# Whole score maxima in four steps over three banks, two score banks, and a reordered routing tail

## The chip, the cores and the metric

The kernel runs on one core of one Trainium2 chip, in one launch. The metric is the device time of that launch in microseconds (us); lower is better. All tensors are float32.

## The reference, cut to what matters

There are 2 sequences of 1024 tokens with 256 features, and a context of 77 tokens for each. The input is normed and is the source of the latents; here the queries come from the 1024 tokens, and the keys and values from the 77 context tokens together with the 1024 tokens, 1101 keys in all. There are 16 heads of 64.

```
q = lat @ Wq ;  k, v = split(concat([x, lat]) @ Wkv)
attn = softmax(q k^T * 64**-0.5) ;  x = x + (attn @ v) @ Wout
xn = layernorm(x)
shared = (silu(xn @ sg) * (xn @ su)) @ sd
scores = l2norm(xn) @ l2norm(centroids).T        # 8 groups, 32 experts
experts of the best 4 groups, of these the best 4 (+ bias), gates = softmax of their scores
routed = sum over the 4 experts of gate * FFN_e(xn), each expert taking its first 320 tokens
out = x + shared + routed
```

## The kernel before

**Numbers in two halves.** Most products are taken in a fast float32 form (F32R) with each operand split into a high part, written by ScalarE (a Copy), and a low part, written by VectorE (a subtraction). A product is then three matmuls: high by high, high by low, low by high.

**Blocks.** The attention runs in 8 turns `T` of 4 blocks `d`: a block is a pair of heads (`pp = d // 2`) with 512 queries (`d % 2`). A turn handles two head pairs of one sequence. Inside a block each of the two heads `h` has 9 slots, one for each 128 keys (`kt`). A slot `("st", d, h, kt)` is two matmuls into a bank of `ps_st` (L906, L910); ScalarE takes the exponential out of the bank (L1569), and GpSimd adds it to a running sum of the row (`add`, L725). The second score matmul also brings in minus the maximum of each query's row. `ps_st` has three banks, used in turn, so a score waits for the exponential of three scores before.

**Maxima.** The maximum over all 1101 keys has to be known before a head's first score. So the scores of that head are computed once more ahead, in 6 steps `("max", d, h, i)`: two matmuls of 370 keys by 128 queries into the two banks of `ps_m` (L883), and one VectorE reduction of 2 x 369 values into two columns of `piece_max` (L1279). There are 12 pieces for a head, three to each 128 queries. A step waits until the reduction of the step before has emptied both banks (`max_done`). `("neg", d, h)` reduces the 12 partial maxima to 4 (L1285), and `("row", d, h)` turns them into a row with a matmul (L889) and a masking on VectorE (L1292). The second head's maxima are taken in the first half of its own block (`own_max`), the next block's first head's in the second half (`next_max`).

**Order of the work.** Every engine walks one list, `PLAN`, which `whole_plan()` writes out by hand, and issues its own part of each event, in that order; semaphores tie the parts together. `turn_slots()` gives the events after each slot of a block: the projections of the next head pair (`k`, `q`, with their `hi` parts on ScalarE and `lo` parts on VectorE), `v`, the products with the values (`av`, L921), the row sums (`sum`, L928, and a VectorE reciprocal, L1296), the norm on GpSimd (`norm`, L730) and the output product (`out`, L941). Blocks with odd `d` project keys (`project`), those with even `d` only the next queries. `extra_events()` puts the work of other stages in: second sequence, and the norm, scores and routing of token groups 0 and 1, spread over VectorE.

**Two more banks.** All other products that leave TensorE go through a ring of two banks, `ps_t`: job number `jn` uses `ps_t[jn % 2]`, and `bank_free`, `job_filled` and `job_done` wait on its two pairs of semaphores. Together this is 2 + 3 + 1 (`ps_o`) + 2 banks, all eight.

**The tail.** After the last block come four chunks of 512 tokens of the shared FFN (`up` into `ps_m` and `ps_st`, `silu` on ScalarE, `hid`, `lowh` on VectorE, `down`), and between them the routing of token groups 2 and 3: norms (`norm_a`, `norm_b`), transposes (`turned`), `score`, `top`, `mask`, `best`, `hot`, `pos`, `places`, and 16 scatters of rows each on GpSimd (`scat`, L742). In the order before, all of group 2's routing and the start of group 3's lie before `("down", 0)`. Behind the list, SyncE waits for the scatters and loads the first expert's rows (`feed(0, 0, False)`); TensorE transposes them (`turn_rows(0, 0)`, L986). Then the loop over 32 experts runs, each an `up` (L780) and a `down` (L817, L811).

Of the kernel before, what the change touches and what calls it, by code (L numbers as in the profile page):

```python
# [12 lines left out]
P = 128  # L13
# [31 lines left out]
MAX_STEPS = 6  # L45
# [3 lines left out]
def turn_slots():  # L49
# [3 lines left out]
    for d in range(QUADS):  # L53
# [8 lines left out]
        def own(*ev):  # L62
            return ev, 0
# [10 lines left out]
        def project_k(i):  # L74
# [7 lines left out]
        own_max = [own("max", d, 1, i) for i in range(MAX_STEPS)] + [own("neg", d, 1)]  # L82
        next_max = [nxt("max", n, 0, i) for i in range(MAX_STEPS)] + [nxt("neg", n, 0)]
        out = [old("out", prev, i) for i in range(2)]
        after = {(0, 1): own_max[1:2],
                 (0, 4): own_max[4:5],
                 (0, 6): own_max[5:],
                 (0, 8): [own("row", d, 1), next_max[0], old("sum", prev)],
                 (1, 1): [],
                 (1, 2): [old("norm", prev), next_max[1]],  # L90
                 (1, 3): first_values + [next_max[2]],
                 (1, 4): [out[0], next_max[3]]}
        if project:
            after[0, 0] = [own_max[0]] + project_k(0)
            after[0, 1] += [k_low[0]]
            after[0, 2] = project_k(2) + [own_max[2], k_low[2]]
            after[0, 3] = project_k(1) + [own_max[3], k_low[1]]
            after[0, 5] = project_q() + [q_again] + last_values + [q_low]
            after[1, 5] = [nxt("v", pp, 0), next_max[4]]
            after[1, 6] = next_max[5:] + more_values + [nxt("row", n, 0), out[1]]  # L100
# [19 lines left out]
def extra_events():  # L120
# [84 lines left out]
    put(30, 1, 7, "end", ("ws", 0))  # L205
    c(31, ("wl", 0))
    put(31, 0, 6, "end", ("wload", 1))
    put(31, 1, 5, "end", ("ws", 1))
    put(31, 1, 6, "end", ("wl", 1), ("wload", 2))
    put(31, 1, 7, "end", ("stat_a", 2), ("stat_b", 2))  # L210
# [4 lines left out]
def whole_plan():  # L215
# [5 lines left out]
              ("max", 0, 0, 1), ("max", 0, 0, 2), ("v", 0, 1), ("max", 0, 0, 3), ("max", 0, 0, 4), ("v", 0, 2),  # L221
              ("max", 0, 0, 5), ("neg", 0, 0), ("row", 0, 0)]
# [4 lines left out]
    for T in range(TURNS):  # L227
        for slot in slots:
            more = extra.get((T,) + slot[0][0][1:], [])
            for n, (ev, back) in enumerate(slot):  # L230
                place = "row" if ev[0] == "row" else "mid" if n == len(slot) - 1 else None
                plan += [(new, T) for at, new in more if at == place]
                if 0 <= T - back < TURNS:
                    plan.append((ev, T - back))
                elif T == 0 and ev[0] == "out":
                    plan.append((("cen", ev[2]), 0))
# [11 lines left out]
    def last(c):  # L248
        return [("high", c, HIDS - 1), ("lowh", c, HIDS - 1), ("down", c), ("accout", c)]

    tail = av + [("up", 0, 0), ("norm_a", 2), ("norm_b", 2), total, ("silu", 0, 0), ("up", 0, 1), ("turned", 2, 0),
                 ("turned", 2, 1), ("hid", 0, 0), norm, ("silu", 0, 1), ("low", 2, 0), ("low", 2, 1), ("hid", 0, 1),
                 ("ws", 2), ("wl", 2), ("norm_c", 2), ("up", 0, 2), ("score", 2), ("scored", 2)] + outs
    tail += [("silu", 0, 2), ("high", 0, 0), ("lowh", 0, 0), ("hid", 0, 2), ("stat_a", 3), ("stat_b", 3), ("root", 3),
             ("high", 0, 1), ("lowh", 0, 1), ("top", 2), ("up", 0, 3), ("mask_a", 2), ("mask_b", 2), ("silu", 0, 3),
             ("hid", 0, 3), ("high", 0, 2), ("lowh", 0, 2), ("norm_a", 3), ("norm_b", 3), ("best_a", 2), ("best_b", 2),
             ("turned", 3, 0), ("turned", 3, 1), ("high", 0, 3), ("lowh", 0, 3), ("hot_a", 2), ("hot_b", 2),
             ("hot_c", 2), ("gexp", 2), ("low", 3, 0), ("low", 3, 1), ("norm_c", 3), ("pos", 2), ("score", 3),
             ("gates", 2), ("places_a", 2), ("places_b", 2), ("scored", 3)] + scats[2]
    tail += [("down", 0), ("accout", 0)] + hidden(1, 0) + [("top", 3), ("mask_a", 3), ("mask_b", 3)] + hidden(1, 1)  # L260
    tail += [("best_a", 3), ("best_b", 3), ("gexp", 3), ("hot_a", 3)] + hidden(1, 2) + [("hot_b", 3), ("hot_c", 3)]
    tail += hidden(1, 3) + [("pos", 3), ("gates", 3), ("places_a", 3), ("places_b", 3)] + scats[3] + last(1)
    tail += hidden(2, 0) + hidden(2, 1) + hidden(2, 2) + hidden(2, 3) + last(2)
    for ht in range(HIDS):
        tail += hidden(3, ht) + ([("ws1", ht)] if ht < WPIECES else [])
    tail += last(3)
# [3 lines left out]
JOB_KINDS = ("k", "q", "v", "row", "sum", "out", "cen", "zt", "turned", "score", "pos")  # L270


def xattn_moe(nc, x, ctx_in, ln_m_g, ln_m_b, ln_l_g, ln_l_b, Wq, Wkv, Wout, group_c, expert_c, e_bias,
# [33 lines left out]
    jobs = 0  # L307
    for ev, T in PLAN:
        if ev[0] in JOB_KINDS:
            JOB[ev, T] = jobs  # L310
            jobs += 1
# [6 lines left out]
    PADS = jobs % 2  # L318
    TURNED_IN = [T for ev, T in PLAN if ev[0] == "turned" and ev[2] == DT - 1]
    J_EXPERT = jobs + PADS  # L320
# [18 lines left out]
    with ExitStack() as stack:  # L339
# [194 lines left out]
        def exp_of(T, d, h, kt):  # L534
            return T * ST_T + SCORES.index(("st", d, h, kt)) + 1 + 3
# [1136 lines left out]
```

## Time and profile before

| | us |
|---|---|
| median of 3 runs | 1708.82 (1708.56 to 1709.96) |
| the profiled execution | 1708.1 |
| its span, first to last instruction | 1706.4 |
| TensorE matmul busy | 1520.7 (89%) |
| VectorE busy | 1053.5 (62%) |
| ScalarE busy | 797.0 (47%) |
| GpSimd busy | 936.3 (55%) |

The attention blocks fill 54 to 1165 us of the span, the tail 1165 to 1284, and the expert loop the rest. TensorE matmuls are pipelined: a row's duration overlaps with the next row's, so the pitch from start to start is what one costs. A bracket at the end of a row is the idle time of the engine before it, with what ended it.

### The profile page before, as it was taken

To read this page: it belongs to the slowest core of one execution; us is meant where nothing else is said; L and a number is where in the kernel's file an instruction comes from. 1 tells how busy PE (TensorE), PEld (TensorE's weight loads), DVE (VectorE), ACT (ScalarE), POOL (GpSimd) and SP (SyncE) were. 2 spreads that over 40 slices of the span, in tenths; PEclk is the share of its full clock that TensorE was granted. 3 is DMA by queue.
4 is the path that set the end of the run, shared out by engine and by line. 5 is a ranking of instruction groups with operands and counts; after the bars stand their busy time and mean duration, and the time that the engine had idled before them with its cause. 6 is when DMAs were issued, how large, how long until landed. Compare 5 with 4: busy or idle time off the path is not lost.

```text
span 1706.4 us, 24003 instructions
## 1 busy us (share of the span) xinstructions
PE 1520.7 (89%) x8086; PEld 1070.6 (63%) x8086; DVE 1053.5 (62%) x1770; ACT 797.0 (47%) x1501; POOL 936.3 (55%) x747
## 2 busy tenths in 40 slices
PE   3798999998989989899899998987789999999995
PEld 3465555555555556555565555544678999999995
DVE  6556666576565656667666676565645666666662
ACT  3344444444444435544354443444225566666663
POOL 4456666666565665666557677784432343333433
PEclk8899999999999999999999999998798999999998
DMA  3032440000000000000001010111225676666664
GB/s 99 12 77 68 89 97 10 23 14 10 14 10 23 14 10 23 14 10 14 10 23 30 26 31 23 30 45 56 72 92 176 171 196 166 184 181 167 192 170 93
DMA packets 99283, 117.94 MB, mean 69 GB/s; under 512 B 10595, under 2 KB 78181, under 8 KB 99173
## 3 DMA queue, kind: packets, MB, share of 16 engines
q1 hardware_dynamic: 82149, 96.97, 19.4%
q0 software_dynamic: 17056, 19.97, 6.0%
q8 instruction: 44, 0.72, 0.2%
q14 instruction: 34, 0.28, 0.0%
HBM read 74.93 MB, written 35.06 MB: 64 GB/s over the span
## 4 chain that ended last, share of the span: by engine, by line
PE 67%; DVE 17%; POOL 6%; ACT 6%; issue 2%; DMA 0%; SPq 0%; POOLq 0%; DVEq 0%; ACTq 0%
PE ps_o L921 10%; DVE piece_max L1279 9%; PE ps_t L780 9%; PE ps_m L780 8%; PE ps_m L883 8%; PE ps_st L780 8%; POOL arena L725 5%; PE ps_st L906 4%; PE ps_t L941 4%; PE ps_st L910 3%; PE ps_st L817 2%; PE ps_o L817 2%; ACT arena_r L1546 2%; PE ps_t L986 2%; PE ps_t L889 2%
## 5 line engine op out<-in xcount | busy, mean ns | idle before, releaser
L725 POOL TENSOR_TENSOR arena<-arena 128x512 f32<-128x512 f32 (+1 forms) x512 | 662.0, 1294 | 388.9 <-ACT arena L1569 350.7
L1569 ACT ACTIVATE arena<-ps_st 128x512 f32<-128x512 f32 (+1 forms) x576 | 328.0, 597 | 492.3 <-PE ps_st L910 473.2
L1279 DVE TENSOR_REDUCE piece_max<-ps_m 128x2 f32<-128x738 f32 x384 | 353.2, 920 | 223.9 <-PE ps_m L883 221.3
L755 POOL DMA_INDIRECT acc_rows<-arena,ids x96 | 150.7, 1570 | 291.2 <-ACT arena L1629 263.5
L883 PE MATMUL ps_m<-arena_r 128*128 128x370 f32 x768 | 220.4, 368 | 76.5 <-DVE piece_max L1279 69.9
L921 PE MATMUL ps_o<-arena 128*64 128x512 f32 (+1 forms) x1152 | 272.3, 608 | 0.0
L906 PE MATMUL ps_st<-arena_r 128*128 128x512 f32 (+1 forms) x576 | 242.1, 420 | 0.7 <-ACT arena L1569 0.7
L883 PEld LDWEIGHTS ps_m<-arena_r 128*128 128x128 f32 x768 | 130.2, 191 | 175.2 <-DVE piece_max L1279 148.6
L910 PE MATMUL ps_st<-arena_r 68*128 68x512 f32 (+2 forms) x576 | 229.7, 399 | 0.4 <-DVE arena_r L1292 0.4
L921 PEld LDWEIGHTS ps_o<-arena 128*64 128x64 f32 (+1 forms) x1152 | 75.1, 138 | 145.1 <-issue 138.1
L780 PE MATMUL ps_m<-arena_r 128*128 128x320 f32 (+1 forms) x864 | 163.9, 325 | 1.2 <-DVE arena_r L1431 1.2
L780 PE MATMUL ps_st<-arena_r 128*128 128x320 f32 (+1 forms) x864 | 160.2, 321 | 0.0
L906 PEld LDWEIGHTS ps_st<-arena_r 128*128 128x128 f32 (+1 forms) x576 | 107.2, 186 | 60.6 <-issue 51.7
L780 PEld LDWEIGHTS ps_m<-arena_r 128*128 128x128 f32 x864 | 135.8, 190 | 12.3 <-issue 8.5
L780 PEld LDWEIGHTS ps_st<-arena_r 128*128 128x128 f32 x864 | 138.0, 190 | 4.1
L1419 DVE TENSOR_TENSOR arena<-arena,ps_st 128x320 f32<-128x320 f32 x128 | 61.9, 484 | 126.1 <-ACT arena L1604 126.1
L1405 DVE TENSOR_TENSOR arena_r<-arena,arena_r 128x1024 fp32r<-128x1024 f32 x93 | 113.7, 1222 | 15.8 <-ACT arena_r L1591 12.5
L910 PEld LDWEIGHTS ps_st<-arena_r 68*128 68x128 f32 (+2 forms) x576 | 107.0, 186 | 11.8 <-DVE arena_r L1292 1.4
L780 PE MATMUL ps_t<-arena_r 128*128 128x512 f32 x384 | 105.9, 413 | 7.1 <-DVE arena_r L1269 5.2
L1296 DVE RECIPROCAL arena<-ps_t 128x512 f32<-128x512 f32 x32 | 106.8, 3337 | 1.2 <-PE ps_t L928 1.2
L1604 ACT ACTIVATE arena<-ps_m 128x320 f32<-128x320 f32 x128 | 56.4, 440 | 103.5 <-PE ps_st L780 101.3
L1591 ACT ACTIVATE arena_r<-arena 128x1024 fp32r<-128x1024 f32 x93 | 98.4, 1058 | 0.0
(183 smaller groups left out, 1859.3 us busy)
## 6 DMA issues: line engine op xcount, KB each, us to landing
arena<-in_L_ffn_wg_dram SPq DMA_DIRECT2D x32, 512.0 KB, 4.5
arena<-in_L_ffn_wu_dram SPq DMA_DIRECT2D x32, 512.0 KB, 6.2
arena<-in_L_ffn_wd_dram SPq DMA_DIRECT2D x32, 512.0 KB, 4.0
x_slots<-route SPq DMA_DIRECT2D x5, 2176.0 KB, 12.9
arena<-x_slots SPq DMA_DIRECT2D x32, 272.0 KB, 2.7
arena_r<-arena_r SPq DMA_DIRECT2D x30, 275.2 KB, 4.0
arena<-in_L_xattn_Wkv_dram SPq DMA_DIRECT2D x32, 128.0 KB, 2.4
arena<-x_slots SPq DMA_DIRECT2D x32, 68.0 KB, 2.4
```

What stands on the lines that cost most here:

```text
L725: pool.tensor_tensor(total, probsT[0:rows, h, 0, :] if kt == 1 else total, probsT[0:rows, h, kt, :], ALU.add).then_inc(added, 1)
L755: pool.indirect_dma_start(out=dst[:, :], in_=y_sb[par][:, c, 0:w], in_offset=None, compute_op=ALU.add, out_offset=bass.IndirectOffsetOnAxi ...
L780: mm = pe.matmul(ps, a, m, start=(n == 0), stop=(n == len(pairs) - 1))
L883: mm = pe.matmul(ps_m[:, bank_m, 0:PIECE_W + 1], q1[h][:, c:c + P], k1[pp][h][:, lo:lo + PIECE_W + 1], start=True, stop=True)
L906: pe.matmul(ps_st[0:rows, n % 3, :], k1[pp][h][:, r], q1[h][:, c:c + 512], start=True, stop=False)
L910: pe.matmul(ps_st[0:rows, n % 3, :], k2[pp][h][kr, r], q2[h][kr, c:c + 512], start=False, stop=True).then_inc(st_ready, 1)
L921: mm = pe.matmul(ps_o[ROWK[h], :], vals[0:rows, d // 2, kt, ROWK[h]], probsT[0:rows, h, kt, :], start=(kt == 0), stop=(kt == KT_N - 1), sk ...
L1279: dve.tensor_reduce(piece_max[:, :, :].rearrange("p a k -> p (a k)")[:, 2 * i:2 * i + 2], ps_m[:, :, 0:PIECE_W], AX.X, ALU.max).then_inc(m ...
L1296: dve.reciprocal(rinv[:, :], bank[:, :]).then_inc(free, 1)
L1405: dve.tensor_tensor(ws_lo[slot][piece], w_raw[slot][:, piece * W:(piece + 1) * W], ws_hi[slot][piece].bitcast(F32), ALU.subtract).then_inc ...
L1569: act.activation(probsT[0:rows, h, kt, :], ps_st[0:rows, n % 3, :], ACT.Exp).then_inc(exp_done, 1)
L1591: act.activation(ws_hi[slot][piece], w_raw[slot][:, piece * W:(piece + 1) * W], ACT.Copy)\
```

## The change

The three pieces of a row of 128 queries go into three banks in one step, and one VectorE reduction over two dimensions (3 x 369 values to 1 value, negated) writes the final column straight into `neg`; `piece_max`, `neg` and its semaphore are gone, and a head has 4 steps. `ps_m` has three banks and `ps_st` two, so a score waits for the exponential of two scores before. The places of the steps in a block change. The routing of groups 2 and 3 uses its own ring of two banks (`ps_m[:, 2, :]` and `ps_o`). In the tail the routing steps are set among more of the FFN work: `("down", 0)` and `("up", 1, 0)` come ahead of group 3's norm and of group 2's `hot` and `pos`, group 3's `hot` comes behind `("down", 1)`. `lowh` of chunk 0 moves from VectorE to GpSimd. The loads and halves of the shared weights, `stat_a` and `stat_b` of group 2, and `("out", 2, 1)` of the last turn come earlier. The first expert's rows are loaded and transposed (`feed`, `erow`) inside the list, behind `("down", 3)` on TensorE and ahead of `("accout", 3)` on SyncE.

```diff
-        own_max = [own("max", d, 1, i) for i in range(MAX_STEPS)] + [own("neg", d, 1)]
-        next_max = [nxt("max", n, 0, i) for i in range(MAX_STEPS)] + [nxt("neg", n, 0)]
+        own_max = [own("max", d, 1, i) for i in range(4)]
+        next_max = [nxt("max", n, 0, i) for i in range(4)]
-        after = {(0, 1): own_max[1:2],
-                 (0, 4): own_max[4:5],
-                 (0, 6): own_max[5:],
-                 (0, 8): [own("row", d, 1), next_max[0], old("sum", prev)],
+        after = {(0, 8): [own("row", d, 1), old("sum", prev)],
                  (1, 1): [],
-                 (1, 2): [old("norm", prev), next_max[1]],
-                 (1, 3): first_values + [next_max[2]],
-                 (1, 4): [out[0], next_max[3]]}
+                 (1, 2): [old("norm", prev), next_max[0]],
+                 (1, 3): first_values + [next_max[1]]}
         if project:
+            after[0, 0] = [own_max[0]] + project_k(0) + [own_max[1], k_low[0]]
             after[0, 2] = project_k(2) + [own_max[2], k_low[2]]
+            after[0, 3] = project_k(1) + [k_low[1]]
+            after[0, 5] = project_q() + [q_again] + last_values + [q_low, own_max[3]]
+            after[1, 4] = [out[0], next_max[2]]
+            after[1, 5] = [nxt("v", pp, 0), next_max[3]]
+            after[1, 6] = more_values + [nxt("row", n, 0), out[1]]
...
         else:
-            after[0, 0] = [own_max[0]] + project_q()
-            after[0, 2] = [own_max[2]]
-            after[0, 3] = [own_max[3]]
-            after[0, 5] = [q_again] + last_values + [q_low]
-            after[1, 5] = [next_max[4]]
-            after[1, 6] = next_max[5:] + [out[1]] + more_values + [nxt("row", n, 0)]
+            after[0, 0] = [own_max[0]] + project_q() + [own_max[1]]
+            after[0, 3] = [own_max[2]]
+            after[0, 5] = [q_again] + last_values + [q_low, own_max[3]]
+            after[1, 4] = [out[0], next_max[2]]
+            after[1, 6] = [out[1], next_max[3]] + more_values + [nxt("row", n, 0)]
...
+    tail += [("silu", 0, 2), ("high", 0, 0), ("lowh", 0, 0), ("scored", 2), ("hid", 0, 2), ("ws", 2), ("wl", 2),
+             ("stat_a", 3), ("stat_b", 3), ("up", 0, 3), ("root", 3), ("high", 0, 1), ("lowh", 0, 1), ("top", 2),
+             ("silu", 0, 3), ("high", 0, 2), ("lowh", 0, 2), ("hid", 0, 3), ("mask_a", 2), ("mask_b", 2),
+             ("high", 0, 3), ("lowh", 0, 3), ("best_a", 2), ("best_b", 2), ("down", 0), ("accout", 0), ("up", 1, 0),
+             ("norm_a", 3), ("norm_b", 3), ("silu", 1, 0), ("hid", 1, 0), ("turned", 3, 0), ("turned", 3, 1),
+             ("hot_a", 2), ("up", 1, 1), ("hot_b", 2), ("hot_c", 2), ("low", 3, 0), ("low", 3, 1), ("gexp", 2),
+             ("norm_c", 3), ("silu", 1, 1), ("high", 1, 0), ("hid", 1, 1), ("lowh", 1, 0), ("score", 3), ("pos", 2),
+             ("up", 1, 2), ("gates", 2), ("places_a", 2), ("places_b", 2)] + scats[2]
+    tail += [("silu", 1, 2), ("high", 1, 1), ("hid", 1, 2), ("lowh", 1, 1), ("up", 1, 3), ("scored", 3), ("top", 3),
+             ("silu", 1, 3), ("high", 1, 2), ("hid", 1, 3), ("lowh", 1, 2), ("mask_a", 3), ("mask_b", 3),
+             ("best_a", 3), ("best_b", 3)] + last(1) + [("hot_a", 3), ("hot_b", 3), ("hot_c", 3), ("gexp", 3)]
+    tail += hidden(2, 0) + hidden(2, 1) + [("pos", 3), ("gates", 3), ("places_a", 3), ("places_b", 3)] + scats[3]
+    tail += hidden(2, 2) + hidden(2, 3) + last(2)
...
-    tail += last(3)
+    tail += last(3)[:-1] + [("feed",), ("erow", 0), ("erow", 1)] + last(3)[-1:]
...
-        ps_m = stack.enter_context(nc.psum_tensor("ps_m", [P, 2, 512], F32))
-        ps_st = stack.enter_context(nc.psum_tensor("ps_st", [P, 3, 512], F32))
+        ps_m = stack.enter_context(nc.psum_tensor("ps_m", [P, 3, 512], F32))
+        ps_st = stack.enter_context(nc.psum_tensor("ps_st", [P, 2, 512], F32))
-        ey_bank = (ps_o, ps_st[:, 2, :])
+        ey_bank = (ps_o, ps_m[:, 2, :])
+        route_bank = (ps_m[:, 2, :], ps_o[:, :])
...
-                    dve.wait_ge(max_ready, T * MAX_T + (d * 2 + h) * MAX_STEPS + i + 1)
-                    dve.tensor_reduce(piece_max[:, :, :].rearrange("p a k -> p (a k)")[:, 2 * i:2 * i + 2],
-                                      ps_m[:, :, 0:PIECE_W], AX.X, ALU.max).then_inc(max_done, 1)
+                    dve.wait_ge(max_ready, T * MAX_T + d * 8 + h * 4 + i + 1)
+                    c = MROW[h].start + i
+                    dve.tensor_reduce(neg[h][:, c:c + 1], ps_m[:, :, 0:PIECE_W], AX.XY, ALU.max, negate=True)\
+                       .then_inc(max_done, 1)
...
+                if kind == "lowh" and ev[1] == 0:
+                    ht = ev[2]
+                    pool.wait_ge(hid_hi_done, ht + 1)
+                    pool.tensor_tensor(hid_lo[:, ht, :], hid32[ht][:, :], hid_hi[:, ht, :].bitcast(F32), ALU.subtract)\
+                        .then_inc(hid_done, 1)
```

## Rows read from the trace of the kernel before

**Rows 1.** The page's first line.

```profile
span 1706.4 us, 24003 instructions
```

**Rows 2.** Groups of instructions: count, busy us, mean ns, idle before.

```profile
L1279 DVE TENSOR_REDUCE piece_max<-ps_m 128x2 f32<-128x738 f32 x384 | 353.2, 920 | 223.9 <-PE ps_m L883 221.3
...
L1285 DVE TENSOR_REDUCE arena_r<-piece_max 128x4 fp32r<-128x12 f32 x64 | 10.6, 166 | 2.2
...
L1363 DVE TENSOR_REDUCE route<-spare 128x128 f32<-128x512 f32 x3 | 3.2, 1053 | 0.0
```

**Rows 3.** TensorE's timeline around one step: start us, us, instruction, idle before.

```profile
546.26 0.39 PE L910 MATMUL ps_st<-arena_r 68*128 68x512 f32 x1
547.22 0.61 PE L883 MATMUL ps_m<-arena_r 128*128 128x370 f32 x2 [0.56 <-DVE piece_max L1279]
547.66 0.39 PE L906 MATMUL ps_st<-arena_r 128*128 128x512 f32 x1
```

**Rows 4.** TensorE's timeline, the maximum rows of two blocks, and one step.

```profile
502.25 0.50 PE L889 MATMUL ps_t<-ident,arena_r 128*128 128x512 f32 x1
...
519.82 0.47 PE L889 MATMUL ps_t<-ident,arena_r 128*128 128x512 f32 x1 [0.49 <-DVE arena_r L1285]
...
536.43 0.50 PE L889 MATMUL ps_t<-ident,arena_r 128*128 128x512 f32 x1
...
554.94 0.47 PE L889 MATMUL ps_t<-ident,arena_r 128*128 128x512 f32 x1 [0.37 <-DVE arena_r L1285]
...
565.99 0.60 PE L883 MATMUL ps_m<-arena_r 128*128 128x370 f32 x2 [0.80 <-DVE piece_max L1279]
...
571.74 0.50 PE L889 MATMUL ps_t<-ident,arena_r 128*128 128x512 f32 x1
```

**Rows 5.** TensorE's timeline, three scores in a row.

```profile
556.69 0.49 PE L906 MATMUL ps_st<-arena_r 128*128 128x512 f32 x1
...
557.73 0.39 PE L906 MATMUL ps_st<-arena_r 128*128 128x512 f32 x1
```

**Rows 6.** ScalarE's timeline, the exponentials of the first two of these scores.

```profile
557.51 1.09 ACT L1569 ACTIVATE arena<-ps_st 128x512 f32<-128x512 f32 x2 [2.24 <-PE ps_st L910]
```

**Rows 7.** VectorE's timeline: low query half and last maximum; a reciprocal of row sums.

```profile
517.13 1.39 DVE L1272 SCALAR_TENSOR_TENSOR arena_r<-ps_t,arena_r 64x512 fp32r<-64x512 f32 x2 [2.61 <-ACT arena_r L1546]
518.55 0.93 DVE L1279 TENSOR_REDUCE piece_max<-ps_m 128x2 f32<-128x738 f32 x1
...
556.89 3.33 DVE L1296 RECIPROCAL arena<-ps_t 128x512 f32<-128x512 f32 x1
```

**Rows 8.** TensorE's timeline, the output product of the last full block.

```profile
1155.28 1.10 PE L941 MATMUL ps_t<-wout_sb,arena 128*128 128x256 f32 x4 [2.30 <-POOL arena L730]
```

**Rows 9.** TensorE's timeline, the tail: long waits, and `down` work at two speeds.

```profile
1191.52 1.94 PE L947 MATMUL ps_t<-ident,kvT 128*128 128x128 f32 x8 [9.34 <-DVEq L1327]
1199.56 0.79 PE L960 MATMUL ps_t<-route,lower 128*128 128x128 f32 x2 [6.09 <-DVE arena_r L1341]
...
1203.85 8.46 PE L817 MATMUL ps_t<-arena_r 128*128 128x256 f32 x48
...
1228.25 0.76 PE L960 MATMUL ps_t<-route,lower 128*128 128x128 f32 x2 [4.80 <-DVEq L1140]
...
1272.34 3.10 PE L817 MATMUL ps_t<-arena_r 128*128 128x256 f32 x24 [0.17 <-DVE x_sb L1391]
1281.25 1.90 PE L986 MATMUL ps_t<-ident,arena 128*128 128x128 f32 x6 [5.82 <-DMA arena<-x_slots]
1284.39 1.96 PE L780 MATMUL ps_m<-arena_r 128*128 128x320 f32 x6 [1.24 <-DVE arena_r L1431]
```

**Rows 10.** Stretches: busy us of PE, PEld, DVE, ACT, POOL, then PEclk, DMA share, GB/s.

```profile
1204.00:1208.00 4.00, 4.00 (x20) 4.00 (x20) 0.32 (x1) 0.00 (x0) 2.95 (x3) 0.50 0.20 72
```

**Rows 11.** Groups: VectorE's and GpSimd's low halves in the tail.

```profile
L1084 DVE TENSOR_TENSOR arena_r<-arena,arena_r 128x512 fp32r<-128x512 f32 x16 | 11.0, 686 | 4.0 <-ACT arena_r L1491 3.7
...
L733 POOL TENSOR_TENSOR arena_r<-arena,arena_r 128x1024 fp32r<-128x1024 f32 x1 | 2.4, 2350 | 2.3 <-ACT arena_r L1576 2.3
```

More of the change, by code:

```diff
@@ L232, in whole_plan @@
                 plan += [(new, T) for at, new in more if at == place]
-                if 0 <= T - back < TURNS:
+                late = (ev, T - back) == (("out", LAST_D - 1, 1), LAST_T)
+                if 0 <= T - back < TURNS and not late:
                     plan.append((ev, T - back))
+                    if (ev, T - back) == (("out", LAST_D - 1, 0), LAST_T):
+                        plan.append((("out", LAST_D - 1, 1), LAST_T))
                 elif T == 0 and ev[0] == "out":
@@ L249, in last @@
         return [("high", c, HIDS - 1), ("lowh", c, HIDS - 1), ("down", c), ("accout", c)]
[L251 to L263, printed above, removed]
+    tail = av + [("up", 0, 0), ("norm_a", 2), ("norm_b", 2), total, ("silu", 0, 0), ("hid", 0, 0), ("up", 0, 1),
+                 ("turned", 2, 0), ("turned", 2, 1), norm, ("silu", 0, 1), ("low", 2, 0), ("low", 2, 1), ("norm_c", 2),
+                 ("hid", 0, 1), ("up", 0, 2), ("score", 2)] + outs
@@ L264, in whole_plan @@
     for ht in range(HIDS):
         tail += hidden(3, ht) + ([("ws1", ht)] if ht < WPIECES else [])
-    tail += last(3)
+    tail += last(3)[:-1] + [("feed",), ("erow", 0), ("erow", 1)] + last(3)[-1:]
     return plan + [(ev, LAST_T) for ev in tail]
-JOB_KINDS = ("k", "q", "v", "row", "sum", "out", "cen", "zt", "turned", "score", "pos")
+ROUTE_KINDS = ("turned", "score", "pos")
+JOB_KINDS = ("k", "q", "v", "row", "sum", "out", "cen", "zt", "erow") + ROUTE_KINDS
 def xattn_moe(nc, x, ctx_in, ln_m_g, ln_m_b, ln_l_g, ln_l_b, Wq, Wkv, Wout, group_c, expert_c, e_bias,
@@ L825, in _ @@
                     jn = JOB[ev, T]
-                    bank = ps_t[jn % 2]
+                    bank = bank_of(jn)
                     bank_free(pe, jn)
+                    if jn == ROUTE_RING + 1:
+                        pe.wait_ge(o_free, TURNS * O_T + 1)
                 if kind == "zc":
@@ L861, in _ @@
                                                       kvT_hi[:, k, lo:lo + w], kvT_lo[:, k, lo:lo + w])]
-                    product(bank[:, 0:w], pairs).then_inc(job_ready[jn % 2], 1)
+                    product(bank[:, 0:w], pairs).then_inc(ready_of(jn), 1)
                 if kind == "v":
@@ L969, in _ @@
                        lambda k: hT_lo[:, k, a * 512:(a + 1) * 512], a * HT)
+                if kind == "erow":
+                    if a == 0:
+                        pe.wait_ge(rows_in[0], 48)
+                    for c, (lo, rows) in enumerate(CAP_TILES):
+                        mm = pe.transpose(bank[:, lo:lo + rows], xg[0][0:rows, c, a * P:(a + 1) * P], ident[0:rows, 0:rows])
+                    mm.then_inc(ready_of(jn), 1)
                 if kind == "down":
@@ L1203, in _ @@
                     jn = JOB[ev, T]
-                    bank, free = ps_t[jn % 2], job_free[jn % 2]
+                    bank, free = bank_of(jn), free_of(jn)
                 if kind == "kv":
@@ L1244, in _ @@
                     jn = JOB[("zt", a), T]
-                    bank, free = ps_t[jn % 2], job_free[jn % 2]
+                    bank, free = bank_of(jn), free_of(jn)
                     job_filled(dve, jn)
@@ L1263, in _ @@
                     jn = JOB[ev[1:], T]
-                    bank, free = ps_t[jn % 2], job_free[jn % 2]
+                    bank, free = bank_of(jn), free_of(jn)
                     lo, w = ((0, 512), (512, 512), (S, CT))[i]
@@ L1372, in _ @@
                     places_b(a)
+                if kind == "erow":
+                    dve.wait_ge(xe_hi_done, a + 1)
+                    dve.tensor_tensor(xe_lo[:, a, :], bank[:, 0:CAP], xe_hi[:, a, :].bitcast(F32), ALU.subtract)\
+                       .then_inc(free, 1)
                 if kind == "hid":
@@ L1379, in _ @@
                        .then_inc(gu_free, 1)
-                if kind == "lowh":
+                if kind == "lowh" and a:
                     low_hid(a * HT + ev[2])
@@ L1497, in _ @@
                     jn = JOB[ev, T]
-                    bank, free = ps_t[jn % 2], job_free[jn % 2]
+                    bank, free = bank_of(jn), free_of(jn)
                 if kind == "kv":
```

174 lines of the change are left out of this document (84 added, 90 removed).

## The prediction, made before the changed kernel ran

> **What bounds the kernel now.** I read the page first: TensorE is busy for 89% of the 1706.4 us span [rows 1], so what can be won is its idle time, or matmuls taken away. The change takes none away: 12 matmuls of 370 columns for each head before and after. So I looked for where TensorE waits. The groups by line name the main one: 384 reductions of 738 values, 920 ns each, and the matmul line that they release (L883) waits for them [rows 2]. The timeline shows the mechanism. After a score pair TensorE has nothing to issue: the pair started at 546.26 and takes 0.23 us of issue, the next step starts at 547.22, so 0.73 us are lost, and the first matmuls after a wait start 0.44 us apart rather than 0.34, another 0.10 [rows 3]. A step's cycle is 1.63 us: 0.65 from the first matmul to the start of the reduction, 0.93 for it, 0.05 back.
>
> Such waits recur with the plan. I cut the attention at the maximum rows (L889); this gives four segments for two blocks: A from 502.25 to 519.82 (own maxima of a block that projects keys, 17.57 us), B to 536.43 (16.61), C to 554.94 (own maxima of the other kind, 18.51), D to 571.74 (16.80), 69.49 us a pair [rows 4]. Adding up the gaps in TensorE's issue in them, with 0.1 for each restart, gives 9.4 us: about 2.5 in A, 0.8 in B, 3.5 to 3.9 in C, 2.5 in D. There are 16 pairs. The rest of TensorE's idle time is in the tail: 9.34, 6.09, 4.80, 5.82 and 1.24 us, 27.3 together [rows 9].
>
> **The reduction.** The trace has no reduction over two dimensions. From 12 values (166 ns) to 738 (920 ns) a value costs 1.04 ns [rows 2], so 1107 values take 166 + 1095 x 1.04 = 1300 ns. Below, only the fixed part could go: 1.14 us. Above, the nearest row whose inner stride is not one is L1363, 1053 ns for 512 values, or 1.77 ns a value, which would make 2.1 us. The inner dimension here is contiguous as in L1279, and that reduction also steps from bank to bank, so I take 1.30.
>
> **The new cycle.** A step is 3 matmuls (0.51 us of issue), and the next may start at 0.65 + 0.17 + 1.30 + 0.05 = 2.17 us. So TensorE needs 1.66 us of other work between steps, where it had 0.46 (one score) against a need of 1.3. VectorE's own work falls slightly: 4 x 1.30 against 6 x 0.93 + 0.17.
>
> **The lost score bank.** Two scores back to back are free, the third now waits for the first's exponential. It starts at 556.69, the third at 557.73 [rows 5]; the first of the two exponentials ends near 558.06 (they start at 557.51 and two take 1.09) [rows 6]. With two banks the third starts at 558.1 or so, 0.4 later, 0.5 with the restart. Triples stand open in four places a pair: after each row sum (B and D), at (1, 7), (1, 8), (0, 0) in A, and at (0, 1) to (0, 3) in C. That is 2 us a pair, or 32 us over 16 pairs, and it is in the sums below.
> The Trainium skill warns of this edit: its page Trainium Kernel Development and Optimization, Best Practices, says that consistent bubbles can mean that PSUM ran out. By that rule taking a score bank away makes new bubbles, and the row above agrees for triples only; at every score it would be the second rival.
>
> **The segments after.** A: step 1 comes behind one projection (1.4 us), 0.25 short; step 2 is 0.34 short; the ring of `ps_t` holds the last key projection about 0.4; then the last maximum must wait for the low query half. Before, that half runs from 517.13 and the maximum follows it at 518.55 [rows 7], with 0.93 + 0.17 us; now it is 1.30, so the row comes 0.2 later behind the same chain. With restarts and the triple: 2.2 lost, gain 0.3. B: the reciprocal of 3.33 us [rows 7] holds the first reduction to about 5 us behind the row, but one score and the products with values (2.7 us of issue) now stand between, which hides it. Left are the triple and 0.35 before step 2, as much as the 0.8 of before; two interruptions by a step fewer, at 0.1 each: gain 0.2. C: step 1 is 0.35 short with its restart, the triple 0.5, and the last score and the row wait 0.7 (the low query half ends as late as before), against 3.4 without the extra work of this turn: gain 1.85. D: the triple and 0.35 before step 2 against 2.5: gain 1.7. Sum 4.05 a pair; 15 or 16 of each segment give 65 us.
>
> I do not take all of it. From the second half of the attention on, VectorE also carries the norms and routing of groups 0 and 1, and a late start of a longer reduction costs more than of a short one: 15% off, 55. And GpSimd gets no less to do. In D its norm ends some 8.3 us behind the row, TensorE now reaches the output product at 8.1. In the last two turns scatters stand in its queue too, and the last block already waits 2.30 there [rows 8]; each microsecond saved ahead of it comes back as wait. I take 5 us off. Before the first block, 4 longer steps in place of 6 short ones at a low clock give 3. Attention: 53 us.
>
> **The tail.** Today TensorE stops 9.34 us for group 3's norm and 6.09 for group 2's counts, then 4.80 for group 3's counts, while matmuls of later chunks, which need none of this, stand behind them in the list [rows 9]. The new order puts `down` 0 and the next `up` there. What waits then: `down` 0 needs the third weight piece and `lowh` from GpSimd, whose 1024-wide subtraction takes 2.35 us and a 512-wide add 1.3, behind each other, where VectorE takes 0.69 [rows 11]; I count 4.6. Group 3's score needs a route bank that `low` frees: 1.1. `down` 1 needs the last low half, which stands behind `mask` and `best` on VectorE: 3.3. `down` 2 waits 1.0 behind `places`. At the end the first rows are already there, so the 5.82 + 1.24 become about 2.2 (transpose, two copies' latency). 27.3 becomes 12.2: 15 us. SyncE issues the rows before the last `accout` instead of behind it; that store is waited for by the adds alone, which start 15 us later. The second expert's weights go out at about the same point and have an `up` and a `down` to land.
>
> TensorE's clock stood at 0.50, its 1.2 GHz level, in this stretch [rows 10], after the idle 9.34 and 6.09, and again after 4.80 and 5.82. 48 `down` matmuls took 8.46 us there and 24 took 3.10 at full clock, so 2.3 us were lost in this one run [rows 9]. With the scores, transposes, the second such run and the first expert's `up` I estimate 11. The longest wait left is 3.3 us, so I take 8 of it. Tail: 23 us.
> The Trainium skill (TensorE: Matmul & The Clock Gate, Part 1) says that throttled is the default and activity releases it; by that rule all 11 come back if the waits left are short, and none if they are not. The rows above agree with the direction only.
>
> **Sum.** 1708.1 (profiled execution, 1.7 outside its span) - 53 - 23 = 1632; the median is 0.7 above it: 1633.
>
> **The rivals.**
> Reduction at the strided pace (4%): 2.1 us in place of 1.30. Seven steps a pair are exposed (three in A, one in B, two in C, one in D), so 0.81 x 7 x 16 = 90 us come on top: 1723, slower than before. It turns slower from a reduction of 1.30 + 76 / 112 = 1.98 us. For it: three separate regions read as one. Against: L1279 does this with two at 1.04 ns.
> Other queues become the bound (18%): ScalarE's exponentials stand behind its 0.6 us copies with one bank less of slack, and GpSimd's norm behind its adds. If each block loses 0.9 us more in this way, 28 us go: 1661. For it: ScalarE's four copies of a query block and GpSimd's wait in rows 8. Against: both are busy about half the time.
> The tail stays bound by VectorE's chain (8%): only the first rows' part is won, 8 of 23: 1648.
> Everything holds (12%): 65 + 3 in the attention and 27 in the tail: 1614.
> The forecast (58%), by itself 1622 to 1646.
>
> **How the numbers follow.** A measurement here can't tell under 0.2% (3.4 us) from no change. All cases but the strided pace are faster; with 2% for that one ending level and 4% slower, faster has 0.94. The range 1607 to 1672 holds the forecast, the tail and queue rivals and most of the good one; the strided pace and what lies beyond the ends are the 2 in 10 left out.
>
> **What would show it.** The reduction's mean: 1.30. Idle before the maximum matmuls, now 0.56 to 0.80 a time, seen about seven times a pair at 0.2 to 0.5. The third score of a triple 0.4 late, released by ScalarE. Pairs of blocks of about 65 us between rows. In the tail no wait above 4 us, PEclk at 1.00 through most of it, and under 3 us from the last `down` to the first expert. The forecast is wrong if the pair stays above 67 us (then look at who releases the output product), or if the waits in the tail only move to `down`.

## The result, and the profile after

| | before | after |
|---|---|---|
| median, us | 1708.69 (1705.45 to 1709.96, 4 runs) | 1647.66 (1647.04 to 1650.48, 4 runs) |
| ratio, 95% interval | | 0.9649, 0.9631 to 0.9666 |
| span | 1706.4 | 1645.3 |
| before the first row of maxima | 53.6 | 50.2 |
| first to last such row (63 segments) | 1092.4 | 1049.6 |
| last row to the first expert matmul | 138.4 | 124.3 |
| expert loop | 422.0 | 421.2 |

The change saves 61 us, where the prediction had 76: 46.2 ahead of the last row (53 predicted), 14.9 behind it (23 predicted), 14.1 of them before the first expert and 0.8 in the expert loop. The page's first line of the changed kernel, and its groups by line (columns as in [rows 2]); its reduction is L1307, the maximum matmuls L909, the scores L932 and L936, the exponential L1590:

```profile
span 1645.3 us, 23810 instructions
...
L1307 DVE TENSOR_REDUCE arena_r<-ps_m 128x1 fp32r<-128x1107 f32 x256 | 334.2, 1306 | 179.4 <-PE ps_m L909 175.4 <-DVE spare L1260 0.2
```

The whole maximum costs 1306 ns, so a value costs what it did in [rows 2]. What TensorE waited for (us in total, times, longest):

```profile
PE ps_st L932 <- ACT arena L1590: 27.8, 90, 1.0
PE ps_m L909 <- DVE arena_r L1307: 23.1, 22, 1.8
...
PE ps_t L841 <- DVE arena_r L1111: 5.2, 4, 3.5
```

The first line is new: these are the waits that two score banks make, 0.3 us a time. Before, the waits of the maximum matmuls, now the second line, stood at the head:

```profile
PE ps_m L883 <- DVE piece_max L1279: 69.9, 128, 1.0
```

TensorE's timeline over the pair of blocks that [rows 4] shows for before, cut at the rows of maxima (L915):

```profile
481.38 0.50 PE L915 MATMUL ps_t<-ident,arena_r 128*128 128x512 f32 x1
...
498.81 0.47 PE L915 MATMUL ps_t<-ident,arena_r 128*128 128x512 f32 x1
...
514.92 0.50 PE L915 MATMUL ps_t<-ident,arena_r 128*128 128x512 f32 x1
...
532.28 0.39 PE L915 MATMUL ps_t<-ident,arena_r 128*128 128x512 f32 x1
...
547.38 0.50 PE L915 MATMUL ps_t<-ident,arena_r 128*128 128x512 f32 x1
```

A is 17.43 us (predicted 17.27), B 16.11 (16.41), C 17.36 (16.66), D 15.10 (15.10). This pair is 66.0 us; 65.4 was predicted. But this D is one of the good ones. Over all blocks:

| segment | before, sum | after, sum | gain | predicted, before the deductions |
|---|---|---|---|---|
| A (16) | 278.7 | 276.6 | 2.1 | 4.8 |
| B (15) | 247.9 | 244.1 | 3.8 | 3.0 |
| C (16) | 293.6 | 267.7 | 25.9 | 29.6 |
| D (16) | 272.2 | 261.2 | 11.0 | 27.2 |

A part of C's gain is the clock. Two C segments of the kernel before, of 21.06 and 21.08 us, hold a stretch in which the granted clock was 0.50, TensorE's 1.2 GHz level, and one of the changed kernel, of 18.83 us, does; set against their neighbours of 18.5, 18.1 and 17.4 us this makes about 4 of the 25.9 us. The two stretches of before (columns as in [rows 10]):

```profile
474.90:481.60 6.70, 6.32 (x16) 3.10 (x18) 2.70 (x4) 2.74 (x5) 4.52 (x4) 0.50 0.00 0
966.40:973.10 6.70, 6.49 (x16) 2.36 (x16) 3.68 (x16) 2.13 (x4) 4.71 (x4) 0.50 0.06 21
```

D is 15.1 us where nothing disturbs it and 16.1 to 18.1 in eleven of sixteen blocks (in the first of them the clock also stood at 0.50 for 3.4 us). The timeline of VectorE in a disturbed one (start, us, instruction, idle before):

```profile
267.62 2.67 DVE L1074 TENSOR_SCALAR route<-x_sb,mv,rstd 128x256 f32<-128x256 f32 x2
270.43 1.31 DVE L1307 TENSOR_REDUCE arena_r<-ps_m 128x1 fp32r<-128x1107 f32 x1
```

and of TensorE and GpSimd in the same place:

```profile
268.01 0.78 PE L909 MATMUL ps_m<-arena_r 128*128 128x370 f32 x3
...
271.80 0.78 PE L909 MATMUL ps_m<-arena_r 128*128 128x370 f32 x3 [1.68 <-DVE arena_r L1307]
```

```profile
267.57 1.28 POOL L749 TENSOR_TENSOR arena<-arena 128x512 f32<-128x512 f32 x1
268.81 1.32 POOL L744 TENSOR_TENSOR arena<-arena 128x512 f32<-128x512 f32 x1
```

The maxima are in their banks at 268.8, but VectorE is in the `zs` step (L1074) until 270.3, and the next step waits 1.68 us. The two `zs` took 1.81 us before; they are longer now. Why, the last experiments show.

The tail, TensorE's timeline, the waits that are left:

```profile
1109.63 1.96 PE L967 MATMUL ps_t<-wout_sb,arena 128*128 128x256 f32 x8 [2.40 <-POOL arena L749]
...
1138.62 1.35 PE L841 MATMUL ps_t<-arena_r 128*128 128x256 f32 x6 [2.12 <-POOL arena_r L752]
...
1148.13 5.13 PE L841 MATMUL ps_t<-arena_r 128*128 128x256 f32 x24 [1.65 <-DVE x_sb L1417]
...
1177.32 6.65 PE L841 MATMUL ps_t<-arena_r 128*128 128x256 f32 x30 [3.45 <-DVE arena_r L1111]
...
1221.69 1.18 PE L1000 MATMUL ps_t<-ident,arena 128*128 128x128 f32 x6 [0.74 <-DMA arena<-x_slots]
1224.12 1.78 PE L804 MATMUL ps_m<-arena_r 128*128 128x320 f32 x6 [1.24 <-DVE arena_r L1397]
```

Nothing above 3.45 us, where [rows 9] had 9.34, 6.09, 5.82 and 4.80: behind the output product all waits of the stretch add up to 14.9 us against 30.0. But the clock hardly came back. Stretches, columns as in [rows 10]:

```profile
1140.00:1151.00 11.00, 7.45 (x31) 6.87 (x32) 7.32 (x24) 2.76 (x4) 3.61 (x3) 0.50 0.00 1
1163.00:1167.00 4.00, 4.00 (x14) 3.39 (x14) 3.49 (x16) 0.00 (x0) 0.00 (x0) 0.59 0.00 0
1177.00:1183.00 6.00, 5.68 (x25) 5.52 (x26) 1.54 (x4) 1.03 (x1) 4.47 (x6) 0.50 0.29 105
```

It stood at 0.50 from 1139.0 to 1152.7, right behind the wait of 2.12 us and through those of 1.14, 0.79 and 1.65; from 1162.9 to 1166.3, behind one of 1.40 us; and from 1176.6 to 1183.4, around the end of the 3.45. Not every such wait was followed by a fall: the one of 2.40 us at 1109.63 was not. In its stretches at the low level TensorE is busy for 22.4 us, the start of the first expert included, and for 25.7 before; at half speed that is worth about 2 us, not the 8 predicted.

### The profile page after: what moved, and what is told of

The parts are those of the page before. It is cut to its first block, busy times and chain, and to the rows that moved or that the text cites. A ratio compares the mean times of both kernels' runs of the same rounds, so it can differ in the third digit from the quotient of the medians.

```text
span 1645.3 us, 23810 instructions
## 1 busy us (share of the span) xinstructions
PE 1513.9 (92%) x8086; PEld 1067.2 (65%) x8086; DVE 1050.6 (64%) x1574; ACT 796.0 (48%) x1501; POOL 940.0 (57%) x751
## 4 chain that ended last, share of the span: by engine, by line
PE 72%; DVE 15%; ACT 6%; POOL 3%; issue 2%; DMA 1%; ACTq 0%; SPq 0%; DVEq 0%; POOLq 0%
PE ps_o L947 13%; PE ps_t L804 8%; PE ps_m L909 8%; PE ps_m L804 8%; PE ps_st L804 7%; PE ps_st L932 6%; DVE arena_r L1307 5%; PE ps_st L936 5%; ACT arena L1590 3%; PE ps_m L841 3%; PE ps_o L841 3%; PE ps_t L967 2%; DVE arena L1318 2%; PE ps_t L1014 2%; PE ps_t L954 2%
## 5 line engine op out<-in xcount | busy, mean ns | idle before, releaser
L1590 ACT ACTIVATE arena<-ps_st 128x512 f32<-128x512 f32 (+1 forms) x576 | 327.3, 596 | 463.2 <-PE ps_st L936 430.3
L1307 DVE TENSOR_REDUCE arena_r<-ps_m 128x1 fp32r<-128x1107 f32 x256 | 334.2, 1306 | 179.4 <-PE ps_m L909 175.4
L932 PE MATMUL ps_st<-arena_r 128*128 128x512 f32 (+1 forms) x576 | 247.9, 430 | 27.9 <-ACT arena L1590 27.8
L947 PE MATMUL ps_o<-arena 128*64 128x512 f32 (+1 forms) x1152 | 268.5, 601 | 0.0
L936 PE MATMUL ps_st<-arena_r 68*128 68x512 f32 (+2 forms) x576 | 229.7, 399 | 1.9 <-DVE arena_r L1314 1.9
L909 PE MATMUL ps_m<-arena_r 128*128 128x370 f32 x768 | 194.7, 362 | 31.0 <-DVE arena_r L1307 23.1
L909 PEld LDWEIGHTS ps_m<-arena_r 128*128 128x128 f32 x768 | 130.1, 192 | 118.3 <-DVE arena_r L1307 65.6
L932 PEld LDWEIGHTS ps_st<-arena_r 128*128 128x128 f32 (+1 forms) x576 | 106.9, 186 | 106.7 <-ACT arena L1590 84.2
L936 PEld LDWEIGHTS ps_st<-arena_r 68*128 68x128 f32 (+2 forms) x576 | 107.0, 186 | 12.1 <-DVE arena_r L1314 3.4
## 6 DMA issues: line engine op xcount, KB each, us to landing
x_slots<-route SPq DMA_DIRECT2D x5, 2176.0 KB, 12.9
```

Of the source, the lines that this page charges most:

```text
L909: mm = pe.matmul(ps_m[:, piece, 0:PIECE_W + 1], q1[h][:, c:c + P], k1[pp][h][:, lo:lo + PIECE_W + 1], start=True, stop=True)
L932: pe.matmul(ps_st[0:rows, n % 2, :], k1[pp][h][:, r], q1[h][:, c:c + 512], start=True, stop=False)
L936: pe.matmul(ps_st[0:rows, n % 2, :], k2[pp][h][kr, r], q2[h][kr, c:c + 512], start=False, stop=True).then_inc(st_ready, 1)
L947: mm = pe.matmul(ps_o[ROWK[h], :], vals[0:rows, d // 2, kt, ROWK[h]], probsT[0:rows, h, kt, :], start=(kt == 0), stop=(kt == KT_N - 1), sk ...
L1307: dve.tensor_reduce(neg[h][:, c:c + 1], ps_m[:, :, 0:PIECE_W], AX.XY, ALU.max, negate=True)\
L1590: act.activation(probsT[0:rows, h, kt, :], ps_st[0:rows, n % 2, :], ACT.Exp).then_inc(exp_done, 1)
```

## The experiments

All ratios are to the kernel before, measured beside it on the same chip. The changed kernel, measured again beside `e6`, `e7` and `e8`: 1650.67 us, 0.9656 (0.9621 to 0.9690).

> The changed kernel as it is, on the same chip as the three runs after it, which are compared with it: 1647.7 us.

**The two halves apart.** `e1` has the new maxima, banks and block plan with the old tail, `e2` the old maxima with the new tail and its ring (third bank of `ps_st` and `ps_o`).

> The kernel before with the changed maxima, banks and slots of the attention, but its own tail, its own ring for routing and its own loading of the first expert's rows. Theory (the two traces cut at the maximum rows): the attention gave 46 of the 61 us (3.4 before the first row, 42.8 between the first and the last row), the rest 15. So 1662 us. Rival (the prediction's split, scaled): the tail gave its 23 us and the attention only 38, so 1671. If the two parts help or hinder each other, this run and the next do not add up to 61.

> The kernel before with the changed tail, the routing ring (third score bank and ps_o), and the early rows of the first expert, but its own attention. Theory: 15 us won, 1694 us; TensorE's clock still falls to its 1.2 GHz level in the tail, three times. Rival (the prediction): 23 us won, of which 8 from the clock, 1686.

Measured: 1664.59, ratio 0.9753 (0.9733 to 0.9774), and 1698.44, 0.9945 (0.9927 to 0.9962). Gains 43 and 9.4 us, 8 less than both together. By stretches they do add up: `e1` has 1048.2 us between the rows (44.2 saved), `e2` 125.5 behind them (12.9 saved). What `e2` loses is in its attention, 1098.7 us against 1092.4, and in each of the eight segments that differ by more than 1 us the granted clock was 0.50 for a while in one of the two kernels. Five segments of `e2` are 1.1 to 1.6 us longer, and each holds 3.4 us at that level; the last is 2.3 us longer (16.6 against 14.2) and holds 6.8, where the changed kernel, with the same moved statistics and no such stretch, takes 14.7. The other way round, two C segments of the kernel before, those shown above, are 2.5 and 1.5 us longer than in `e2`. Two of the stretches in `e2`:

```profile
407.10:410.50 3.40, 3.40 (x8) 1.57 (x10) 0.93 (x1) 1.58 (x4) 2.35 (x3) 0.51 0.00 0
1141.00:1147.60 6.60, 6.27 (x15) 2.95 (x15) 2.78 (x3) 1.79 (x3) 6.13 (x6) 0.50 0.11 39
```

Why the clock falls more often in this execution of `e2` than in that of the kernel before, no run shows.

**The lost score bank, and how many steps are exposed.** `e4` is the changed kernel with the third 370 keys written over the second and left out of the maximum, so that the reduction reads 738 values; `e3` has in addition three score banks and two for the maxima, as before. Both leave a third of the keys out of the maximum.

```diff
-mm = pe.matmul(ps_m[:, piece, 0:PIECE_W + 1], ...
+mm = pe.matmul(ps_m[:, min(piece, 1), 0:PIECE_W + 1], ...
-dve.tensor_reduce(neg[h][:, c:c + 1], ps_m[:, :, 0:PIECE_W], AX.XY, ...
+dve.tensor_reduce(neg[h][:, c:c + 1], ps_m[:, 0:2, 0:PIECE_W], AX.XY, ...
# e3 alone:
-ps_m [P, 3, 512], ps_st [P, 2, 512]
+ps_m [P, 2, 512], ps_st [P, 3, 512]
```

> The changed kernel, but the third piece of 370 keys is written over the second in its bank and left out of the maximum (so the reduction takes two banks, 738 values), and the bank set free goes back to the scores, three in turn. Its twin, the next run, is the same with two score banks. Theory: the lost score bank costs what the trace shows, 90 waits for ScalarE at 0.44 us of issue, of which those just ahead of a maximum row are hidden by it: the twin is 25 to 30 us slower than this. Rival 1 (the prediction's count): 4 open triples a pair at 0.5, 32 us. Rival 2: the waits only move to the maximum rows, under 8 us. Absolute: about 1597 us by the theory.

> The twin: the changed kernel with the third piece written over the second and left out of the maximum, so the reduction is 0.93 us rather than 1.31, all else as it is. It prices a microsecond of reduction. Theory: after the change only about four steps a pair are exposed, 4 x 0.38 x 16 = 24 us faster than the changed kernel: 1624 us. Rival (the prediction): seven exposed steps, 43 us, 1605.

Measured: `e3` 1605.16, 0.9402 (0.9384 to 0.9421); `e4` 1611.86, 0.9439 (0.9422 to 0.9456). In kernels with this short reduction the bank is worth 6.7 us, not the 25 to 30 of the expectation nor the 32 of the prediction. TensorE's waits, `e3` first and then `e4`:

```profile
PE ps_t L967 <- POOL arena L749: 30.2, 15, 5.1
```

```profile
PE ps_st L932 <- ACT arena L1590: 29.8, 89, 1.0
...
PE ps_t L967 <- POOL arena L749: 6.0, 7, 2.8
```

The score waits of `e4` are as large as predicted, 89 times 0.33. But take them away and TensorE comes to the output product sooner than GpSimd, which has not finished its norm (L749): 24 us turn up there. A wait ahead of another wait is nearly free. And 0.39 us less on each reduction (920 ns) is worth 36 us, or 5.8 exposed steps a pair (36 / 16 / 0.386): more than the four of `e4`'s expectation, which came out 12 us too slow, and fewer than the seven that the price of the strided rival used. The trace of the changed kernel agrees: 100 of its 256 steps, 6.2 a pair, start within 0.15 us of the end of the reduction before; in `e4` 38 do.

**What disturbs C and D.** `e6` moves the two VectorE steps of the second sequence beside the row of slot (1, 6), eight blocks in all.

```diff
-        a(6 + 2 * i, ("zs", i))
+        b(6 + 2 * i, ("zs", i))
-        d(7 + 2 * i, ("zl", i))
+        b(7 + 2 * i, ("zl", i))
```

> The changed kernel with two steps of the second sequence's norm on VectorE moved: `zs` (two scalings of 0.94 us) from behind slot (1, 3), ahead of a maximum, to (1, 6) ahead of the row, and `zl` from (1, 8) to (1, 6) of the same block. Theory: the changed kernel has lost the slack that hid such work; D took 16.7 instead of 15.1 us in the four blocks with `zs`, C 17.36 instead of 16.27 in the four behind `zl`, so 6.4 + 4.4 = 11 us come back: 1637. Rival: the excess comes from GpSimd's queue and stays: 1646 to 1648.

Measured: 1640.63, 0.9589 (0.9556 to 0.9622), 10 us below the changed kernel measured beside it, though the intervals touch. The segments show the gain where it was expected: the four D go from 16.7 to 15.1, the four C from 17.3 to 16.3, 10.6 us together. In the profiled execution the 63 segments are only 6.8 us shorter, since one C and one D of `e6` are 3.0 and 1.5 us longer; the granted clock was 0.50 there, for 6.8 and 3.4 us.

**Low halves on VectorE again.** `e7` gives `lowh` of chunk 0 back.

> The changed kernel with the low halves of chunk 0 back on VectorE (0.69 us each instead of 1.30 on GpSimd). In the trace VectorE's small operations there take 1.1 to 1.3 us beside them instead of 0.2 to 0.3. Theory: GpSimd's subtraction holds VectorE up as well as being slower, so the move to GpSimd bought nothing: `down` 0 starts earlier, 1 to 3 us won, 1645 to 1647. Rival: VectorE's chain through top and best of group 2 is what ends last at `down` 0, and four more operations of 0.69 us on it cost 2 to 3 us: 1650.

Measured: 1648.40, 0.9644 (0.9608 to 0.9679), 2.3 us below the changed kernel measured beside it and within the noise; last row to first expert 124.0 us against 125.7. No verdict, at most 2 us.

**GpSimd's norm one slot earlier.** `e8`, meant to end the waits at the output product:

```diff
-                 (1, 1): [],
-                 (1, 2): [old("norm", prev), next_max[0]],
+                 (1, 1): [old("norm", prev)],
+                 (1, 2): [next_max[0]],
```

> The changed kernel with GpSimd's norm of the output one slot earlier, ahead of one row sum addition of 1.29 us. Theory: GpSimd's norm is now the last to be ready in the even blocks of the last two turns and in the last block (waits of 1.53 and 2.40 us for it), so 4 to 6 us come back: 1643. Rival: the norm waits for the reciprocal there, or another engine is ready as late, under 2 us: 1646 or more.

Measured: 1668.96, 0.9758 (0.9726 to 0.9790): 18 us slower, so the forecast fell, though its own term is there: 122.2 us behind the last row against 125.7. The 16 D sum to 291.1 us, 30 more than in the changed kernel. VectorE and GpSimd in one of them, by the timeline:

```profile
135.86 3.36 DVE L1286 TENSOR_TENSOR arena_r<-arena,arena_r 128x512 fp32r<-128x512 f32 x1
139.15 1.30 DVE L1307 TENSOR_REDUCE arena_r<-ps_m 128x1 fp32r<-128x1107 f32 x1
```

```profile
132.25 3.96 POOL L744 TENSOR_TENSOR arena<-arena 128x512 f32<-128x512 f32 x3
136.18 1.27 POOL L749 TENSOR_TENSOR arena<-arena 128x512 f32<-128x512 f32 x1
137.41 2.93 POOL L744 TENSOR_TENSOR arena<-arena 128x512 f32<-128x512 f32 x2
```

The subtraction of the `w` low half, two operands from SBUF, took 0.91 us in this block of the changed kernel; here 3.36, while GpSimd's norm next to it took 1.27 and the two additions behind it 2.93 (1.28 each in the median). Over the run (duration min, median, max), changed kernel and `e8`:

```profile
L1286 DVE TENSOR_TENSOR arena_r<-arena,arena_r x16: 697/946/3006, 18.1 to 1006.5; 128x512 fp32r<-128x512 f32 x16
```

```profile
L1286 DVE TENSOR_TENSOR arena_r<-arena,arena_r x16: 747/3386/5423, 18.1 to 1032.3; 128x512 fp32r<-128x512 f32 x16
```

A third of what D loses comes by way of the clock. In this block TensorE waits 2.12 us for the late reduction, and then the clock was 0.50 for 3.4 us:

```profile
142.00:145.20 3.20, 3.20 (x10) 2.58 (x9) 2.41 (x3) 0.61 (x2) 1.27 (x1) 0.50 0.83 196
```

Eight D segments hold such a stretch that has no counterpart in the changed kernel; where two D are alike otherwise, the one with it takes 18.5 us and the one without 17.3, so about 10 of the 30 us are the slower clock.

**The same with `w` out of the way.** `e9` is `e8` with that subtraction just ahead of the row of slot (1, 6); for `d == 2` alike.

```diff
-            after[1, 1] = [own("w", 1)] + after[1, 1]
+            after[1, 6].insert(-1, own("w", 1))
```

> As in the kernel of 1668.96 us (ratio 0.9758), GpSimd's product with the reciprocal stands one slot earlier than in the changed kernel, but the subtraction of the `w` low half (VectorE, L1286 there) is taken out of slot (1,1) and put just ahead of the row in slot (1,6). Theory (the collision of these two is what cost 18 us: L1286 took a median 3.39 us there and 0.95 us in the changed kernel, and the maximum behind it came late): L1286 falls back to about 1 us where GpSimd has only its additions, the even blocks' second sequence goes to its undisturbed 15.1 us in most blocks (sum of 16 about 250, against 291 there and 262 in the changed kernel), and the time is 1640, ratio 0.960. Rival (the product itself is too early: GpSimd waits for the reciprocal in front of its additions, which hold the exponentials): moving `w` changes nothing, the sum stays near 290 and the time near 1668, ratio 0.976. A third: L1286 collides with the additions in its new place as it did with the product, takes 3 us there, and the row of these blocks comes 2 us late: 16 times 2 us in place of 29, about 1665.

Measured: 1638.63, 0.9585 (0.9557 to 0.9612). The rival that the norm itself is too early is out: the norm is where it was in `e8`, and 30 us are gone, the eight falls of the clock with them. The 16 D sum to 253.8 us, 12 above sixteen clean ones of 15.1; in the changed kernel it is 20, in `e8` 49. Some 5 of the 12 are in the four D with `zs`, whose pair takes 3.2 us here. Behind the last row it is 121.9 us. The subtraction in `e9`:

```profile
L1286 DVE TENSOR_TENSOR arena_r<-arena,arena_r x16: 693/819/1652, 18.6 to 1010.4; 128x512 fp32r<-128x512 f32 x16
```

**Together.** `e10` is `e6` with `w` moved as in `e9`, and the low half of the shared weights' third block two steps earlier in the tail; `e11` is `e10` with the norm of `e8` (its expectation says "the kernel before" for `e10`, its neighbour).

> The changed kernel with three kinds of VectorE's work put elsewhere, GpSimd's product left in its slot: the `zs` and `zl` steps beside the row of slot (1,6), which gave ratio 0.9589 alone; the `w` subtraction just ahead of that row as well; and in the tail the low half of the shared expert's third block of weights two steps earlier (the wait of 3.45 us at 1177.32 in the changed kernel's trace). Theory (what the hand walk missed is VectorE's extra work that the lost slack lays bare): 1641 from the first, 0 to -3 from the second, -2 from the third: 1637, ratio 0.958 (1633 to 1641). Rival (`w` beside `zs` at the same row, and both ahead of a reduction, come too thick): the row is late in 4 blocks by 1 to 2 us, 1645, ratio 0.963.

> The kernel before with GpSimd's product one slot earlier in addition. Theory of the collision: the product now meets no subtraction, so that it gives back what the output product waited for it (0.3 to 1.4 us a block in the even blocks' second sequence of the later blocks, about 6 us in all) instead of costing 18: 1630, ratio 0.954 (1626 to 1634). Rival (the product one slot earlier is harmful by itself): 18 us slower than its neighbour of this call, about 1655, ratio 0.969.

Measured: `e10` 1633.49, 0.9552 (0.9525 to 0.9579); `e11` 1629.36, 0.9533 (0.9505 to 0.9561), the fastest kernel here that takes the whole maximum. Their runs don't overlap (1633.02 to 1634.54 and 1629.10 to 1631.46), though the intervals do. The total of `e10` was right, its terms not: the step in the tail gave nothing (the wait is 3.45 us as before, 125.7 us behind the last row), and `w` gave more than the 0 to 3 us expected, D going from `e6`'s 256.9 to 250.3, because in the last blocks it had collided too (1.7 to 3.0 us there, now 0.7), and because one fall of the clock (1.5 us) is gone. `e11` gains, but not in the even blocks where it was expected: it gains in one place, 121.6 us behind the last row against 125.7: the last output product no longer waits for the norm, 2.09 us in `e10`, and the 3.4 us at 0.50 that followed that wait are gone as well. In the sum of the D segments the two are level (248.4, 250.3).

## Why the prediction was right, and where it was short

1633 was forecast with 1607 to 1672; it is 1648, and the mechanism of the likeliest case holds.

- *The reduction at 1.30 us*: 1.306. The strided rival was out with that row.
- *The segments by hand*: for the pair of [rows 4] right within 0.3 us in A, B and D; C took 17.36 us, 0.7 more than said. C's gain was worked out for a block without extra work, and there it is 1.6 us (17.9 to 16.3) against the 1.85 said; in the four blocks with `zl` it is 1.2. The sum over the attention was 64.6 before deductions, 42.8 is measured, and 16.2 of the missing 21.8 are in D (C lacks 3.7, and without the clock's 4 us it would lack nearly 8). The step that was mis-sized is the deduction for VectorE's other work, "15% off": 10 us, where 21.8 are missing. It was spread over everything, where it falls on few places: the third step of D starts 0.06 us and the fourth 0.06 to 0.10 us behind the reduction before it in nearly every block, so there is no slack left, and what VectorE loses in slots (1, 1) to (1, 3) shows on TensorE. Before, there was some: the fourth of D's six steps started 0.60 us behind the reduction where nothing disturbed it and 0.06 us behind it with `zs`, and the `zs` made D longer by 0.1 us, 16.8 to 16.9, where in the changed kernel they make it longer by 1.6. The price of the strided rival also counted one exposed step in D and three in A; the trace has two in each. `e6`, `e9` and `e10` show that it is this: moved away, the D segments come down by 5, 8 and 11 us in sum.
- *The lost score bank, 32 us*: as a gross price right (90 waits of 0.31 us, and the restarts), as a price of the decision wrong: 6.7 us, measured in kernels with the shorter reduction. The rule quoted from the Trainium skill (Trainium Kernel Development and Optimization, Best Practices: "consistent bubbles can mean SBUF/PSUM ran out") agrees with the 90 new waits; of what they cost it says nothing.
- *GpSimd, 5 us off*: the output product waits 3.9 us for it in the changed kernel, less than the 8.5 of before; the saving did not come back as this wait, since TensorE was held up ahead of it. It is the next bound: with the shorter reduction and three score banks it takes 30 us.
- *The tail, 15 us of waits*: 15.1 measured. *The clock, 8 us*: about 2 in the changed kernel. "The longest wait left is 3.3 us" was right (3.45), the conclusion was not: the clock fell behind waits of 2.12 and 1.40 us as well. This is the second mis-sized term.
- *The rival of the queues* (1661) had the right place, VectorE's and GpSimd's queues in the second half, and named ScalarE and GpSimd instead of VectorE. The rival of the unmoved tail gave 1648 by chance: it saved 8 us in the tail, measured are 14.9.
- *What would show it*: idle time ahead of the maximum matmuls was to be seen seven times a pair at 0.2 to 0.5 us. The trace shows 22 waits, of 1.05 us on average: few and long, as disturbed blocks make them. The other exposed steps start late without idle time that it shows, since a matmul's row lasts longer than its issue.

## What to carry to other kernels

When a reduction holds TensorE up a few times in a block, count its exposed starts, and after the change look at what else stands in VectorE's queue at those starts: work that was hidden behind the old waits is the first to cost. Price a resource that is given up (here a bank) by what would be waited for without it, not by the waits that it causes. Before moving an operation of GpSimd, look at which VectorE operations with all operands in SBUF run at that time; here the move of the GpSimd operation alone cost 18 us, and with the VectorE operation moved as well the two gained about 11. And where two kernels differ by a few microseconds, compare the stretches at the low clock before looking for another cause.

## What the runs showed of the hardware

Some of VectorE's instructions on SBUF are held up for the length of GpSimd's, which mostly keep their time (the additions of the changed kernel take 1.28 us in the median; 5 of 512 take 1.5 to 2.1). A pair of `zs` steps (one SBUF tensor in) takes 0.72 us in `e11`, with GpSimd idle at its start, and 2.67 in the changed kernel beside the norm and an addition; `e11`, VectorE's timeline:

```profile
275.03 0.84 DVE L1286 TENSOR_TENSOR arena_r<-arena,arena_r 128x512 fp32r<-128x512 f32 x1
275.79 0.72 DVE L1074 TENSOR_SCALAR route<-x_sb,mv,rstd 128x256 f32<-128x256 f32 x2
```

In the tail of the changed kernel a conversion of 16 values takes 1.14 us, ending as GpSimd's subtraction ends (1139.79 + 1.26), while a product with one operand in PSUM (L1404) takes its usual 0.69 beside the subtraction before it:

```profile
1136.29 0.69 DVE L1404 TENSOR_TENSOR arena<-arena,ps_st 128x512 f32<-128x512 f32 x1 [1.41 <-POOL arena_r L757]
...
1139.94 1.14 DVE L1122 CAST topf<-top8i 128x16 f32<-128x16 uint32 x1
```

```profile
1136.20 2.37 POOL L752 TENSOR_TENSOR arena_r<-arena,arena_r 128x1024 fp32r<-128x1024 f32 x1
1139.79 1.26 POOL L757 TENSOR_TENSOR arena_r<-arena,arena_r 128x512 fp32r<-128x512 f32 x1 [1.23 <-ACT arena_r L1512]
```

This is what the Trainium skill says of the port pair shared by the two engines (SBUF — State Buffer, "SBUF: two separate sides"): an exclusive lock, which the loser waits out in full, for VectorE instructions with two SBUF inputs or in a two-port mode. The durations here agree; in which mode the `zs` steps and the conversion ran, no trace shows. One thing goes beyond it: in `e8` the subtraction started 0.3 us before the norm, as an addition ended, and still ended behind the norm and about one addition, as if GpSimd, with its next instruction ready, kept the pair each time. That is read from durations only; no run was made for it.
